# A two-layer graph kernel: x centred by TensorE, the residual kept transposed, and every other block transfer issued by GpSimd into slots of its own

## The chip, the cores and the metric

The kernel runs on one core of one Trainium2 chip. The metric is the device time in microseconds (us) of one launch; lower is better. The kernel before is timed in three runs, and one more execution of it is profiled.

## The reference, cut to what matters

N = 8192 nodes have 64 features each. The dense matrix `adj` is 8192 x 8192 float32 (256 MiB) and is used in both layers.

```
h = max(layernorm(x), 0)
x = x + adj @ (h * (u >= 0.1) / 0.9)        # layer 1
h = max(layernorm(x), 0)
x = x + adj @ (h @ W) + b                   # layer 2
```

Layer 2 needs the finished rows of layer 1: its right-hand side for a block of nodes exists only when layer 1 has been summed over the whole row of `adj` for these nodes.

## The kernel before

`adj` is cut into 16 x 16 blocks of 512 x 512 (1024 KB each). Multiplication is done with the features as the stationary operand (128 nodes x 64 features, one half of TensorE's columns) and a piece of a block as the moving one, so that two matmuls, one for each half, run side by side. Row 0 of blocks is done as two half rows of 256 nodes. W is applied at the end, to the sums of layer 2 (`acc`), and not to h.

The order of all the work is a list of 335 **items** that `Order` builds when the program is made; it is numbered from 0. An item of kind `one` is one block (or the half blocks of a pair) for layer 1 and has 2 steps; `ahead` is half a block for both layers and has 2 steps; `both`, `pair` and `mix` do two matmuls of 512 columns for each of four tiles and have 4 steps. Items 0 to 11 are half-row items of row 0 (the first unit of layer 1 is items 0 to 7), item 12 is the first that needs features of layer 2.

A block is not always used once: loaded blocks that are near the diagonal are kept for layer 2. The list of items yields a list of 341 **loads**, numbered from 0 in the order of their first use. `plan` gives each load one of the `SLOTS` places in SBUF: the one whose holder was last used earliest.

```python
    for load in loads:
        load.slot = min(range(SLOTS), key=lambda q: free[q])
        load.before, load.arrived = holder[load.slot], 16 * count[load.slot]
```

SyncE (SP) issues x and u in three parts each, then all loads in their order. Before a load into a slot that had a holder, it waits until TensorE has done the last item that uses the holder (`used`). TensorE waits before the first item of a load until the load has arrived (`block_arrived`). So a load has between its issue and its first use the work of the items between these two; this is called its **lead** here. Queue and list are in order: a load that waits for its slot holds back the ones behind it.

VectorE (DVE), ScalarE (ACT) and GpSimd (POOL) normalise x in nine groups of nodes (mean on DVE, centring on POOL, squares on ACT, the rest on DVE), which gives `features[:, :, 0:64]`. After each unit of layer 1 `unit_of_layer_1` turns the sums back to nodes by rows, adds them to `rows` and makes the features of layer 2 (`h2_ready`). `add_sum` moves finished sums out of PSUM. At the end `finish` multiplies `acc` by W for each of eight pairs of rows.

Of the kernel before, what the change touches and what calls it, by code (L numbers as in the profile page):

```python
# [4 lines left out]
P = 128  # L5
N = 8192
# [12 lines left out]
SLOTS = 14  # L19
# [8 lines left out]
GROUPS = [(0, 1), (1, 2)] + [(k, k + 2) for k in range(2, BLOCKS, 2)]  # L28

PARTS = [(0, 2), (2, 8), (8, BLOCKS)]  # L30
PART_OF = [[n for n, (a, b) in enumerate(PARTS) if a <= k0 < b][0] for k0, _ in GROUPS]
GROUP_OF = {k: g for g, (k0, k1) in enumerate(GROUPS) for k in range(k0, k1)}
BIAS_ROW = 8
# [205 lines left out]
def plan():  # L239
# [11 lines left out]
    for load in loads:  # L251
        load.slot = min(range(SLOTS), key=lambda q: free[q])
# [37 lines left out]
    for q in sorted(sums, key=lambda q: q.last):  # L290
# [3 lines left out]
        q.opens, q.ahead_opens = not halves & opened, q.ahead is not None and q.ahead not in ahead_done  # L294
# [20 lines left out]
def bass_gnn(nc, x, adj, u, w, b, out):  # L315
# [7 lines left out]
    first_ahead = min(ahead_done) // 2  # L323
    joined_by = {s: n + 1 for n, s in enumerate(sorted(ahead_done))}
    END = len(items)

# [11 lines left out]

    def unit_tiles(m):

        return slice(m * HALF_TILES, (m + 1) * HALF_TILES) if m < HALVES else slice((m - 1) * TILES, m * TILES)
# [4 lines left out]
    with ExitStack() as ctx:  # L346
# [9 lines left out]
        rows = sb("rows", [P, N // P, D])  # L356
# [3 lines left out]
        ahead = sb("ahead", [P, max(ahead_done) // 2 - first_ahead + 1, BLK])  # L360
        sums_sb = sb("sums_sb", [D, 2, BLK])
        folded = sb("folded", [D, BLK])

        w_twice = sb("w_twice", [P, D])
        bias = sb("bias", [P, D])

        eps = sb("eps", [P, 2])
        total = sb("total", [P, N // P])
# [4 lines left out]
        dev2 = sb("dev2", [P, TILES])  # L373
        centred2 = sb("centred2", [P, TILES, D])
# [3 lines left out]

        u_sb = acc[:, :, :].rearrange("p a (t d) -> p (a t) d", d=D)
        centred = features[:, :, D:2 * D]  # L380
        x_squares = features[:, :, 0:D]
# [4 lines left out]
        squares = finished[0:D, 0, :]  # L386
        banks = ctx.enter_context(nc.psum_tensor("banks", [P, SUM_BANKS, BLK], f32))

# [4 lines left out]
        bias_arrived = sem("bias_arrived")  # L393
        cleared = sem("cleared")
        warm = sem("warm")
        x_mean = sem("x_mean")
        x_centred = sem("x_centred")
        x_squared = sem("x_squared")
        x_dev = sem("x_dev")
# [26 lines left out]
        def tiles_of(k):  # L426
            return slice(k * TILES, (k + 1) * TILES)

        def group_tiles(g):
            return slice(GROUPS[g][0] * TILES, GROUPS[g][1] * TILES)  # L430

# [443 lines left out]
```

## Time and profile before

| | |
|---|---|
| median of 3 runs | 922.01 us (921.55 to 922.12) |
| profiled execution, its own time | 921.98 us |
| its span, first to last instruction | 920.2 us |
| TensorE busy | 891.7 us (97% of the span) |
| VectorE, ScalarE, GpSimd busy | 261.0, 41.0, 10.6 us |
| HBM read | 360.78 MB, 394 GB/s over the span |
| granted clock of TensorE | 1.000 |

The time of a run holds the span and 1.8 us around it. TensorE is busy in nearly all of the span, so what can be lost or won quickly is the time in which it waits. Matmul durations in rows overlap each other, because they are pipelined and two run side by side; the pace is read from the starts.

### The profile page before, as it was taken

The page shows a single profiled execution, that of the slowest core. Times are in us where ns is not written, and L with a number is a line of the kernel's source. Part 1 is how long each engine was busy: PE and PEld are TensorE (multiplying, and loading weights), DVE is VectorE, ACT ScalarE, POOL GpSimd, SP SyncE. Part 2 cuts the span into 40 slices and gives each one's busy share as a digit, 9 for nine tenths or more (in the row PEclk, how much of TensorE's full clock was granted, in tenths as well). Part 3 has the DMA queues.
Part 4 walks back from the last instruction along what each step waited for, and adds up shares of the span by engine and source line. Part 5 has one row for each costly group of instructions (what it writes and reads, how often), then busy time and mean ns, then how long its engine had stood idle before and what let it go on. Part 6 is the DMA issues. An engine that isn't in the chain of part 4 may idle for free.

```text
span 920.2 us, 10857 instructions
## 1 busy us (share of the span) xinstructions
PE 891.7 (97%) x4616; PEld 408.7 (44%) x4616; DVE 261.0 (28%) x529; ACT 41.0 (4%) x173; POOL 10.6 (1%) x18
## 2 busy tenths in 40 slices
PE   1899999999999999999999999999999999999998
PEld 1545444444444444444444444444444444444443
DVE  6664733323303303030403022030130300300423
ACT  7400000000000000000000000000000000000000
POOL 3100000000000000000000000000000000000000
PEclk9999999999999999999999999999999999999999
DMA  9999999999999999999999999999999999999996
GB/s 360 420 422 421 421 420 421 421 421 363 421 422 420 421 420 420 421 420 415 366 412 376 379 372 389 373 361 402 352 358 371 382 404 398 384 385 406 402 423 240
DMA packets 53200, 363.59 MB, mean 395 GB/s; under 512 B 5744, under 2 KB 6288, under 8 KB 11040
## 3 DMA queue, kind: packets, MB, share of 16 engines
q1 hardware_dynamic: 53056, 362.83, 97.5%
q8 instruction: 37, 0.61, 0.3%
q0 software_dynamic: 96, 0.07, 0.0%
q14 instruction: 11, 0.09, 0.0%
HBM read 360.78 MB, written 2.10 MB: 394 GB/s over the span
## 4 chain that ended last, share of the span: by engine, by line
PE 92%; DMA 6%; SPq 2%; issue 0%; DVE 0%
PE banks L737 45%; PE row_sums L713 37%; DMA blocks<-in_adj 6%; PE banks L731 6%; PE banks L747 3%; SPq L454 1%; PE row_sums L722 1%; PE banks L826 0%; PE finished L795 0%; PE row_sums L795 0%; SPq L437 0%; SPq L436 0%; DVE acc L661 0%; DVE rows L670 0%
## 5 line engine op out<-in xcount | busy, mean ns | idle before, releaser
L737 PE MATMUL banks<-blocks,features 128*64 128x512 f32 x1912 | 665.2, 593 | 0.0
L713 PE MATMUL row_sums<-blocks,features 128*64 128x512 f32 x1696 | 547.8, 592 | 2.0 <-DMA blocks<-in_adj 1.9
L737 PEld LDWEIGHTS banks<-blocks,features 128*64 128x64 f32 x1912 | 221.2, 137 | 214.0 <-issue 213.2
L713 PEld LDWEIGHTS row_sums<-blocks,features 128*64 128x64 f32 x1696 | 192.1, 137 | 203.4 <-issue 195.4
L621 DVE TENSOR_TENSOR acc<-acc,banks 64x512 f32<-64x512 f32 (+1 forms) x112 | 76.9, 687 | 575.5 <-PE banks L737 527.9
L731 PE MATMUL banks<-blocks,features 128*64 128x512 f32 x224 | 98.1, 592 | 0.1
L722 PE MATMUL row_sums<-blocks,features 128*64 128x256 f32 x256 | 32.1, 403 | 23.4 <-DMA blocks<-in_adj 23.4
L747 PE MATMUL banks<-blocks,features 128*64 128x256 f32 x240 | 54.3, 379 | 0.0
L731 PEld LDWEIGHTS banks<-blocks,features 128*64 128x64 f32 x224 | 30.6, 137 | 29.0 <-issue 28.8
L747 PEld LDWEIGHTS banks<-blocks,features 128*64 128x64 f32 x240 | 32.8, 137 | 21.6 <-issue 8.4
L589 DVE TENSOR_TENSOR rows<-rows,finished 32x128 f32<-32x128 f32 (+1 forms) x136 | 37.0, 272 | 4.3
L722 PEld LDWEIGHTS row_sums<-blocks,features 128*64 128x64 f32 x256 | 21.8, 145 | 33.6 <-DVE features L551 20.2
L520 ACT ACTIVATE sums_sb<-row_sums 64x512 f32<-64x512 f32 (+1 forms) x10 | 5.5, 552 | 378.2 <-PE row_sums L713 173.3
L493 ACT ACTIVATE features<-rows,total 128x64 f32<-128x64 f32 x64 | 21.3, 334 | 5.3 <-DVE total L533 5.3
L520 ACT ACTIVATE sums_sb<-ahead 64x512 f32<-64x512 f32 x7 | 4.4, 627 | 344.9 <-DVE ahead L636 344.9
L628 DVE TENSOR_TENSOR ahead<-ahead,banks 64x512 f32<-64x512 f32 x28 | 19.2, 686 | 0.9
L636 DVE TENSOR_TENSOR ahead<-ahead,row_sums 64x512 f32<-64x512 f32 x15 | 10.3, 685 | 21.7 <-PE row_sums L713 21.5
L619 DVE COPY acc<-banks 64x512 f32<-64x512 f32 x16 | 11.0, 689 | 17.7 <-PE banks L737 10.9
L493 ACT ACTIVATION_READ_ACCUMULATOR features<-rows,total 128x1 f32 x64 | 11.9, 186 | 0.0
L583 DVE STREAM_TRANSPOSE finished<-folded 64x512 f32<-64x512 f32 (+1 forms) x17 | 11.7, 687 | 0.6
L542 DVE SCALAR_TENSOR_TENSOR acc<-acc,square 128x512 f32<-128x512 f32 (+1 forms) x9 | 10.8, 1203 | 0.3
L626 DVE COPY ahead<-banks 64x512 f32<-64x512 f32 x15 | 10.3, 688 | 0.5
(40 smaller groups left out, 112.9 us busy)
## 6 DMA issues: line engine op xcount, KB each, us to landing
blocks<-in_adj SPq DMA_DIRECT2D x339, 1024.0 KB, 9.9
out<-rows SPq DMA_DIRECT2D x7, 256.0 KB, 5.6
rows<-in_x SPq DMA_DIRECT2D x1, 1024.0 KB, 11.5
acc<-in_u SPq DMA_DIRECT2D x1, 1024.0 KB, 13.5
blocks<-in_adj SPq DMA_DIRECT2D x2, 512.0 KB, 22.4
rows<-in_x SPq DMA_DIRECT2D x1, 768.0 KB, 7.7
acc<-in_u SPq DMA_DIRECT2D x1, 768.0 KB, 9.5
rows<-in_x SPq DMA_DIRECT2D x1, 256.0 KB, 3.2
```

Of the source, the lines that this page charges most:

```text
L493: nc.scalar.activation(x_squares[:, j, :], rows[:, j, :], ACT.Square, bias=total[:, j:j + 1], accum_out=square[:, j:j + 1]).then_inc(x_squ ...
L542: nc.vector.scalar_tensor_tensor(out=u_sb[:, t, :], in0=u_sb[:, t, :], scalar=DROP, in1=square[:, t].unsqueeze(2).to_broadcast([P, t.stop ...
L583: nc.vector.transpose(squares[:, 0:width(m)], folded[:, 0:width(m)]).then_inc(row_turned, 1)
L589: nc.vector.tensor_tensor(to, to, part[:, :, a, :], ALU.add).then_inc(row_placed, 1)
L619: nc.vector.tensor_copy(mine, banks[at, q.bank, :]).then_inc(sum_added, 1)
L621: nc.vector.tensor_tensor(mine, mine, banks[at, q.bank, :], ALU.add).then_inc(sum_added, 1)
L628: nc.vector.tensor_tensor(mine, mine, banks[at, q.bank, :], ALU.add).then_inc(sum_added, 1)
L713: return nc.tensor.matmul(row_sums[at, t.unit % 2, nodes], features[:, k * TILES + j, 0:D], tile, start=first and t.n == unit_first[t.unit ...
L722: done = nc.tensor.matmul(row_sums[half * D:(half + 1) * D, t.unit % 2, 0:HALF_BLK], features[:, t.k * TILES + j, 0:D], blocks[:, load.slo ...
L731: return nc.tensor.matmul(banks[at, t.sum.bank, nodes], features[:, t.k * TILES + j, 0:D], tile, start=j == t.tiles[0], stop=j == t.tiles[-1])
L737: return nc.tensor.matmul(banks[at, t.sum.bank, nodes], features[:, t.k * TILES + j, D:2 * D], tile, start=t.n == t.sum.first and j == t.t ...
L747: nc.tensor.matmul(banks[0:D, t.sum.bank, nodes], features[:, t.k * TILES + j, D:2 * D], tile, start=j == 0, stop=j == TILES - 1)
```

## The change

The list of items and the list of loads stay as they are. What changes:

- **Queues and slots.** There are 16 slots in place of 14. Loads with an even number go to even slots and are issued by SP, loads with an odd number go to odd slots and are issued by POOL on its own DMA queue, after its set-up. x and u stay on SP's queue, ahead of load 0.
- **Centring.** x comes in transposed (`x1`). TensorE multiplies each 128 x 128 tile of it by a centring matrix, which POOL makes at the start; this turns the tile and takes off the mean in one matmul. 32 of these stand ahead of item 0 in TensorE's program. ACT squares from PSUM in one instruction for 512 columns, DVE sums the squares; POOL's centring, DVE's means and ACT's 64 small squares go.
- **The transposed residual.** The sums of layer 1 are added to `x1` as they are (two adds), then turned into `turned` for the norm; four of the eight placing copies are done by ACT. The buffer `ahead`, its joining adds and ACT's copy of the upper sums go. The bias is added by ACT.
- **Finishing.** A pair is finished with 4 matmuls of 256 columns with W stationary, in place of 16 of 64 columns.

```diff
-SLOTS = 14
+SLOTS = 16
...
     free, holder, count = [-1] * SLOTS, [None] * SLOTS, [0] * SLOTS
-    for load in loads:
-        load.slot = min(range(SLOTS), key=lambda q: free[q])
+    for n, load in enumerate(loads):
+        load.slot = min(range(n % 2, SLOTS, 2), key=lambda q: free[q])
...
+        def load_blocks(engine, turn):
+            for load in loads[turn::2]:
                 if load.before is not None:
-                    sp.wait_ge(used, load.before.until + 1)
+                    engine.wait_ge(used, load.before.until + 1)
...
-                sp.dma_start(to, of).then_inc(block_arrived[slot], 16)
+                engine.dma_start(to, of).then_inc(block_arrived[slot], 16)
...
+            for n, (p0, p1) in enumerate(PARTS):
+                t = slice(2 * p0 * TILES, 2 * p1 * TILES)
+                sp.dma_start(x1[:, p0:p1, :], x[:, p0:p1, :]).then_inc(x_arrived[n], 16)
+                sp.dma_start(u_sb[:, t, :], u[:, t, :]).then_inc(u_arrived[n], 16)
+            load_blocks(sp, 0)
...
+            nc.gpsimd.memset(centring[:, :], 0.0).then_inc(centring_made, 1)
+            pool.wait_ge(centring_made, 1)
+            for n in range(2):
+                half = centring[(1 - n) * D:(2 - n) * D, n * D:(n + 1) * D]
+                nc.gpsimd.memset(half, -1.0 / D).then_inc(centring_made, 1)
+            for n in range(2):
+                pool.wait_ge(centring_made, 3 + n)
+                nc.gpsimd.affine_select(out=centring[:, :], in_=centring[:, :], compare_op=ALU.not_equal,
+                                        fill=1.0 - 1.0 / D, base=(2 * n - 1) * D, pattern=[[-1, 2 * D]],
+                                        channel_multiplier=1).then_inc(centring_made, 1)
+            load_blocks(pool, 1)
...
             def unit_of_layer_1(m):
-                dve.wait_ge(row_copied, m + 1)
                 dve.wait_ge(used, max(unit_last[m]) + 1)
-                lower = row_sums[0:D, m % 2, 0:width(m)]
-                if s in ahead_done:
-                    dve.wait_ge(row_joined, joined_by[s])
-                    if s % 2 == 1:
-                        lower = ahead[0:D, s // 2 - first_ahead, :]
+                if s:
+                    dve.wait_ge(sum_added, ahead_done[s])
+                link2(nc.vector.tensor_tensor(sums_of_row, sums_of_row, row_sums[0:D, m % 2, 0:width(m)], ALU.add))
+                nc.vector.tensor_tensor(sums_of_row, sums_of_row, row_sums[D:P, m % 2, 0:width(m)], ALU.add)\
+                    .then_inc(row_summed, 1)
+                dve.wait_ge(row_summed, m + 1)
                 if m:
-                    dve.wait_ge(row_turned, m)
-                nc.vector.tensor_tensor(folded[:, 0:width(m)], lower, sums_sb[:, m % 2, 0:width(m)], ALU.add)\
-                    .then_inc(row_folded, 1)
-                dve.wait_ge(row_folded, m + 1)
-                if m:
-                    dve.wait_ge(row_placed, m * (D // SQ) * (P // SQ))
-                nc.vector.transpose(squares[:, 0:width(m)], folded[:, 0:width(m)]).then_inc(row_turned, 1)
+                    dve.wait_ge(row_placed, m * (P // SQ))
+                    dve.wait_ge(row_placed_act, m * (P // SQ))
+                nc.vector.transpose(squares[x1_half(s), 0:width(m)], sums_of_row).then_inc(row_turned, 1)
                 dve.wait_ge(row_turned, m + 1)
-                for f in range(D // SQ):
-                    part = squares[f * SQ:(f + 1) * SQ, 0:width(m)].rearrange("p (t a f) -> p t a f", t=tiles, f=SQ)
-                    for a in range(P // SQ):
-                        to = mine[a * SQ:(a + 1) * SQ, :, f * SQ:(f + 1) * SQ]
-                        nc.vector.tensor_tensor(to, to, part[:, :, a, :], ALU.add).then_inc(row_placed, 1)
-                dve.wait_ge(row_placed, (m + 1) * (D // SQ) * (P // SQ))
+                base = x1_half(s).start
+                part = squares[base:base + SQ, 0:width(m)].rearrange("p (t a f) -> p t a f", t=tiles, f=SQ)
+                for a in range(P // SQ):
+                    nc.vector.tensor_copy(turned[a * SQ:(a + 1) * SQ, 0:tiles, 0:SQ], part[:, :, a, :])\
+                        .then_inc(row_placed, 1)
...
-                    mine = ahead[at, q.p - first_ahead, :]
-                    if q.ahead_opens:
-                        nc.vector.tensor_copy(mine, banks[at, q.bank, :]).then_inc(sum_added, 1)
-                    else:
-                        nc.vector.tensor_tensor(mine, mine, banks[at, q.bank, :], ALU.add).then_inc(sum_added, 1)
-            def join_ahead(m):
-                s = row_of(m)
-                at = slice((1 - s % 2) * D, (2 - s % 2) * D)
-                dve.wait_ge(used, max(unit_last[m]) + 1)
-                dve.wait_ge(sum_added, ahead_done[s])
-                mine = ahead[at, s // 2 - first_ahead, :]
-                nc.vector.tensor_tensor(mine, mine, row_sums[at, m % 2, :], ALU.add).then_inc(row_joined, 1)
+                    mine = x1[at, q.p, :]
+                    nc.vector.tensor_tensor(mine, mine, banks[at, q.bank, :], ALU.add).then_inc(sum_added, 1)
...
-            def finish(n, p, tiles):
-                for j in tiles:
-                    for half in range(2):
-                        for row in range(2):
-                            at, nodes = slice(half * D, (half + 1) * D), j * P + half * D
-                            mine = slice(row * D, (row + 1) * D)
-                            done = nc.tensor.matmul(final_banks(n)[at, row, j * D:(j + 1) * D],
-                                                    acc[mine, p, nodes:nodes + D], w_twice[mine, :],
-                                                    start=True, stop=True)
-                done.then_inc(finished_ready, 1)
+            def finish(n, r, c, bank, acc_of):
+                return nc.tensor.matmul(final_banks(n)[c * D:(c + 1) * D, bank, 0:acc_of.shape[1]],
+                                        w_twice[r * D:(r + 1) * D, 0:D], acc_of, start=True, stop=True)
...
+            pe.wait_ge(centring_made, 5)
+            for p in range(PAIRS):
+                pe.wait_ge(x_arrived[PART_OF[p]], 16)
+                if p >= len(centred):
+                    pe.wait_ge(xd_ready, p - len(centred) + 1)
+                for j in range(TILES):
+                    done = nc.tensor.matmul(x_centred_of(p)[:, 2 * j:2 * j + 2, :], x1[:, p, j * P:(j + 1) * P],
+                                            centring[:, :], start=True, stop=True)
+                done.then_inc(x_centred, 1)
```

On TensorE the matmuls of the centring stand at the start of the program. `centring` is the matrix, `x` is the transposed input, `row_sums` takes the sums of layer 1. Before:

```order
L722 MATMUL row_sums<-blocks,features 64x256 [waits block_arrived0,xd_ready]
L722 MATMUL row_sums<-blocks,features 64x256 x7
L722 MATMUL row_sums<-blocks,features 64x256 [waits block_arrived1,xd_ready]
L722 MATMUL row_sums<-blocks,features 64x256 x7
L722 MATMUL row_sums<-blocks,features 64x256 [waits block_arrived2,xd_ready]
```

and in the changed kernel, from the last two pairs of rows that are centred:

```order
L833 MATMUL row_sums<-centring,x 128x128 [waits x_arrived2]
L833 MATMUL row_sums<-centring,x 128x128 x3
L833 MATMUL banks<-centring,x 128x128 [waits xd_ready,x_arrived2]
L833 MATMUL banks<-centring,x 128x128 x3
L710 MATMUL row_sums<-blocks,features 64x256 [waits block_arrived0,xd_ready]
L710 MATMUL row_sums<-blocks,features 64x256 x7
L710 MATMUL row_sums<-blocks,features 64x256 [waits block_arrived1,xd_ready]
```

32 matmuls in groups of four have come in ahead of the first item, the last groups behind the third part of x (`x_arrived2`); the 8 matmuls of each half-row item and their waits are the same.

On SP the program of before begins like this (`rows` and `acc` take x and u, `blocks` the loads):

```order
L436 DMA rows<-in_x 128x512
L437 DMA acc<-in_u 128x512
L436 DMA rows<-in_x 128x1536
L437 DMA acc<-in_u 128x1536
L436 DMA rows<-in_x 128x2048
L437 DMA acc<-in_u 128x2048
L454 DMA blocks<-in_adj 128x2048 x12
L454 DMA blocks<-in_adj 128x1024
```

In the changed kernel SP has the same six, and then only half of the loads:

```order
L468 DMA acc<-in_u 128x2048
L461 DMA blocks<-in_adj 128x2048 x6
L461 DMA blocks<-in_adj 128x1024
L461 DMA blocks<-in_adj 128x2048
L461 DMA blocks<-in_adj 128x2048 [waits used] x7
```

The other half of the loads stands on POOL, behind the making of the centring matrix:

```order
L485 DMA w_twice<-in_wb 64x65
L488 MEMSET centring 128x128
L492 MEMSET centring 64x64 [waits centring_made]
L495 AFFINE_SELECT centring<-centring 128x128
L495 AFFINE_SELECT centring<-centring 128x128 [waits centring_made]
L461 DMA blocks<-in_adj 128x2048 x8
L461 DMA blocks<-in_adj 128x2048 [waits used] x72
```

POOL's first eight loads (1, 3, ... 15) wait for nothing but POOL itself, and x and u are not ahead of them in its queue.

What the two ways of giving out slots do to single loads can be listed from `plan`. The steps of lead are those of the items between the release of the slot (or that of a load ahead of it in its queue, if later) and the first use:

```
load  first used   before: released   steps     changed: released   steps
      by item      after item         of lead   after item          of lead
 80      95           88               12          91                  6
 82      97           91               12          93                  8
 92     108          100               16         106                  2
 94     110          105                8         108                  2
 96     113          107               14         110                  8
108     126          119               14         122                  8
110     128          122               14         124                  8
loads with 8 steps or fewer:            1                              7
loads with 12 steps or fewer:          14                             15
```

## Rows read from the trace of the kernel before

**Rows 1.** The page: span, busy time, the share of the main queue

```profile
span 920.2 us, 10857 instructions
PE 891.7 (97%) x4616; PEld 408.7 (44%) x4616; DVE 261.0 (28%) x529; ACT 41.0 (4%) x173; POOL 10.6 (1%) x18
```

**Rows 2.** Busy time by stretch: PE, PEld, DVE, ACT, POOL, clock, DMA share, GB/s

```profile
0.00:10.00 10.00, 0.00 (x0) 0.00 (x0) 2.92 (x8) 4.84 (x20) 2.73 (x10) 1.00 0.79 274
20.00:30.00 10.00, 9.50 (x70) 6.27 (x68) 9.48 (x16) 9.38 (x54) 3.33 (x4) 1.00 1.01 422
130.00:140.00 10.00, 9.36 (x44) 3.45 (x42) 4.48 (x12) 0.59 (x1) 0.00 (x0) 1.00 1.02 424
140.00:150.00 10.00, 9.46 (x53) 4.60 (x51) 2.82 (x7) 0.30 (x1) 0.00 (x0) 1.00 1.01 422
250.00:260.00 10.00, 9.17 (x44) 2.96 (x44) 1.29 (x4) 0.30 (x1) 0.00 (x0) 1.00 1.01 421
300.00:400.00 100.00, 100.00 (x485) 45.74 (x483) 23.50 (x53) 2.41 (x5) 0.57 (x1) 1.00 1.01 420
800.00:900.00 100.00, 100.00 (x570) 45.36 (x568) 24.06 (x50) 1.19 (x3) 0.00 (x0) 1.00 0.99 401
```

**Rows 3.** The waits of all engines: who waited for whom

```profile
PE row_sums L722 <- DMA blocks<-in_adj: 23.4, 9, 19.2
PE row_sums L713 <- DMA blocks<-in_adj: 1.9, 4, 0.6
```

**Rows 4.** The timeline of PE from 0 to 60 us

```profile
19.20 9.45 PE L722 MATMUL row_sums<-blocks,features 128*64 128x256 f32 x64 [19.20 <-DMA blocks<-in_adj]
29.15 1.95 PE L722 MATMUL row_sums<-blocks,features 128*64 128x256 f32 x16 [0.50 <-DMA blocks<-in_adj]
...
44.04 1.95 PE L722 MATMUL row_sums<-blocks,features 128*64 128x256 f32 x16 [0.52 <-DMA blocks<-in_adj]
46.53 1.95 PE L722 MATMUL row_sums<-blocks,features 128*64 128x256 f32 x16 [0.54 <-DMA blocks<-in_adj]
48.27 0.59 PE L731 MATMUL banks<-blocks,features 128*64 128x512 f32 x1
```

**Rows 5.** The line that issues the loads: time from issue to landing

```profile
L454 SPq DMA_DIRECT2D blocks<-in_adj x341: 327/328/6210, 3.7 to 887.4; - x171
DMA to landing us min/median/max: 4.7/9.9/29.8
```

**Rows 6.** The chain that ended last, 115 to 150 and 205 to 260 us

```profile
143.67 0.21 PE banks L747
...
205.54 1.72 PE row_sums L713 x8
...
245.07 7.85 DMA blocks<-in_adj
252.96 1.94 PE row_sums L713 x8
```

**Rows 7.** DMA view of 0 to 50 us (40 slices of 1.25 us), and a small transfer of POOL's

```profile
GB/s 0 116 264 327 349 363 362 415 419 433 419 426 433 426 426 433 419 426 426 419 419 426 419 419 419 419 419 433 419 419 426 419 413 406 400 446 410 423 419 419
...
bias<-in_b POOLq DMA_DIRECT2D x1, 32.0 KB, 5.3
```

**Rows 8.** The timeline of POOL and of DVE: the set-up, and the last features of a unit

```profile
1.94 0.53 POOL L474 DMA_DIRECT2D w_twice<-in_w  x1
...
22.89 1.04 POOL L480 TENSOR_TENSOR features<-rows,total 128x512 f32<-128x512 f32 x1 [2.23 <-DVE total L533]
...
142.21 0.42 DVE L604 SCALAR_TENSOR_TENSOR features<-centred,square 128x256 f32<-128x256 f32 x1
```

**Rows 9.** The groups by line with shapes apart: a weight load and an add

```profile
L713 PEld LDWEIGHTS row_sums<-blocks,features 128*64 128x64 f32 x1696 | 192.1, 137 | 203.4 <-issue 195.4 <-DMA blocks<-in_adj 6.8
L621 DVE TENSOR_TENSOR acc<-acc,banks 64x512 f32<-64x512 f32 x49 | 33.6, 685 | 190.6 <-PE banks L737 143.2 <-PE row_sums L713 47.4
```

**Rows 10.** The timeline of the end, 880 to 920 us

```profile
894.49 0.69 PE L795 MATMUL row_sums<-w_twice,acc 64*64 64x64 f32 x32
...
895.11 3.65 PE L737 MATMUL banks<-blocks,features 128*64 128x512 f32 x16
...
898.70 0.69 PE L795 MATMUL finished<-w_twice,acc 64*64 64x64 f32 x32
```

More of the change, by code:

```diff
@@ L27 @@
 STEP, BLOCK_LOAD, LANDING, MARGIN, H2_LEAD, ROW_LEAD = 0.858, 2.49, 1.6, 8.0, 8.0, 10.0
[L28 to L33, printed above, removed]
+PARTS = [(0, 1), (1, 4), (4, PAIRS)]
+PART_OF = [n for n, (p0, p1) in enumerate(PARTS) for _ in range(p0, p1)]
 SQ = 32
@@ L293, in plan @@
         assert not halves & opened or halves <= opened
-        q.opens, q.ahead_opens = not halves & opened, q.ahead is not None and q.ahead not in ahead_done
+        q.opens = not halves & opened
         opened |= halves
@@ L322, in bass_gnn @@
     final_end = {pair_end[p]: p for p in finals}
-    first_ahead = min(ahead_done) // 2
-    joined_by = {s: n + 1 for n, s in enumerate(sorted(ahead_done))}
     END = len(items)
+    assert sorted(ahead_done) == list(range(1, BLOCKS))
     last = items[-1]
@@ L355, in bass_gnn @@
         features = sb("features", [P, N // P, 2 * D])
-        rows = sb("rows", [P, N // P, D])
+        x1 = sb("x1", [P, PAIRS, BLK])
         acc = sb("acc", [P, PAIRS, BLK])
[L360 to L365, printed above, removed]
+        centring = sb("centring", [P, 2 * D])
+        w_twice = sb("w_twice", [P, D + 1])
+        bias = w_twice[:, D:D + 1]
         eps = sb("eps", [P, 2])
-        total = sb("total", [P, N // P])
         square = sb("square", [P, N // P])
@@ L487, in _ @@
+            for n in range(2):
[4 more added lines that the diff above has]
+            load_blocks(pool, 1)
         @block.scalar
         def _(act):
-            def squares_x(g):
-                act.wait_ge(x_mean, 2 * g + 2)
-                for j in range(GROUPS[g][0] * TILES, GROUPS[g][1] * TILES):
-                    nc.scalar.activation(x_squares[:, j, :], rows[:, j, :], ACT.Square, bias=total[:, j:j + 1],
-                                         accum_out=square[:, j:j + 1]).then_inc(x_squared, 1)
@@ L595, in unit_of_layer_1 @@
                 nc.vector.tensor_reduce(var, power, AX.X, ALU.add).then_inc(h2_summed, 1)
-                if s == BIAS_ROW:
-                    dve.wait_ge(bias_arrived, 16)
-                if s >= BIAS_ROW:
-                    since = rows[:, slice(0 if s == BIAS_ROW else s * TILES, (s + 1) * TILES), :]
-                    nc.vector.tensor_tensor(since, since, bias[:, :].unsqueeze(1).to_broadcast(
-                        [P, since.shape[1], D]), ALU.add).then_inc(biased, 1)
                 dve.wait_ge(h2_dev, m + 1)
```

226 lines of the change are left out of this document (115 added, 111 removed).

## The prediction

> **What bounds the kernel now.** I read the page first, then the busy time by stretch, the waits of TensorE, and last the places where it waits. The page shows TensorE busy in 891.7 of 920.2 us [rows 1]; by stretch it is at 100.00 of 100 us from 300 us on [rows 2]. So the change can win only in the other 28 us, but it can lose anywhere. Nearly all of TensorE's waiting is on transfers of blocks [rows 3]: 19.2 us until load 0, then a gap in front of each of the items 1 to 11, and four small ones later. In the timeline items 10 and 11 start at 44.04 and 46.53, 2.49 us apart [rows 4], while such an item is 1.72 us of work [rows 6]. 2.49 us is 1024 KB (1.049 MB) at the 422 GB/s of the stretch, where the share of the DMA engines is 1.01 [rows 2]: the transfers are the bound up to 48.27 us, where item 12 starts. From there TensorE has no reserve: its shortfall is 0.64 and 0.54 us at 130 to 150 us and 0.83 us at 250 to 260 us [rows 2], and none later. The reader should take this from it: **whatever makes the first twelve items late by more than about 1.2 us moves the end by the rest, and every new gap behind them moves it by its whole length.**
>
> The last gap has another cause than the first ones. The chain goes from an item that ended at 245.07 through a transfer of 7.85 us to the next item at 252.96 [rows 6]: load 94, with a lead of 8 steps, that is 4 items of 1.72 us, 6.9 us. Its slot came free too late. That is the measure for the table of leads: a load needs 4.7 us from issue to landing at the least, of 341 of them [rows 5], and 7.85 us where others are in flight.
>
> **The start.** SP must bring x and u (4096 KB, 4.19 MB) and then loads 0, 2, ... 10. Up to load 10 that is 4.19 + 6 x 1.049 = 10.49 MB. Before, load 11 needed 4.19 + 12 x 1.049 = 16.78 MB. First I test the working on this: by 6.25 us the first five slices give 1.25 us x (0 + 116 + 264 + 327 + 349) GB/s = 1.32 MB [rows 7]; (16.78 - 1.32) / 0.422 = 36.6 us; 6.25 + 36.6 = 42.9, and the item starts at 46.53 [rows 4], 3.6 us later. That is the lag between the bytes and TensorE (by the same working of load 0 it is 3.7 us).
>
> POOL's set-up ends at 2.5 us [rows 8]; behind it stand three small fills and two selects over 128 columns, each of which I take as at most the 1.04 us of POOL's instruction on 512 columns [rows 8], and the first transfer needs some time to start. I let POOL's queue join at 6.25 us (bounds 4 and 9 us). It has 8 free slots and nothing ahead of them, and its slots are freed again from item 3 on, so it has work all the time. If the engines serve both queues alike, SP gets 211 GB/s. Load 0 is then there at 6.25 + 3.92/0.211 + 3.6 = 28.4 us in place of 19.2, and load 10 at 6.25 + 9.17/0.211 + 3.6 = 53.3 us. Items 10 and 11 are 3.44 us more: item 12 starts at 56.7 us in place of 48.27, **+8.4 us**. The blocks that POOL has brought in meanwhile are of no use to a TensorE that needs the even ones in order. It doesn't depend much on the shares: with a third for POOL, its sixth load (load 11, 6.29 MB at 141 GB/s) is the late one, 6.25 + 44.6 + 3.6 = 54.5 us, and item 12 starts at 56.2.
>
> Do both queues share? POOL's 32 KB transfer of the bias landed in 5.3 us [rows 7], while a block on SP's queue took 9.9 us at the median behind its own kind [rows 5]; it did not stand behind what SP had issued. The Trainium skill says the same ("DMA: Bandwidth & Descriptors", "Queues, rings and completion order": each engine goes round the queues that have work, packet by packet). By that rule the start costs the 8.4 us; by the order of issue it would cost nothing. The same page ("Issuing engines are not separate DMA queues") says that issuing from several engines saves only the issue time; the share of 1.01 with one queue [rows 2] agrees, so I count no gain in rate.
>
> Of the 8.4 us about 1.2 are taken up by the two gaps between 130 and 150 us: **-1.2**.
>
> **The slots.** Loads 92 and 94 have 2 steps of lead, 1.72 us. Each is issued when a TensorE that is one item away from it frees the slot, and no work done elsewhere hides that. The gap is the landing less 1.72 us: 3.0 us with the least landing, 6.1 us with 7.85 us [rows 5, 6]. POOL's queue will be in flight beside it and TensorE's standstill empties the queues, so I take the middle, 4.5 us: **+9.0**. Load 80 has 6 steps, 5.2 us: 0 to 2.7 us, taken as **+1.0**. Four loads (82, 96, 108, 110) have 8 steps, the lead with which load 94 waited 0.8 us before: 0 to 1 us each, **+1.0** together, since two of them come behind gaps in which the queue has caught up. Load 94's old gap goes: **-0.8**. The two further slots deepen the reserve of the odd loads, but the count of short leads goes up, and where leads are long nothing waited before [rows 3].
>
> **What I cost at nothing.** The 32 centring matmuls: the last 16 follow the third part of x, which by the working above has 3.15 MB of SP's queue: 6.25 + 1.83/0.211 + 3.6 = 18.5 us. One is at most two weight loads of 137 ns [rows 9] and a quarter of a half-row item's columns in time, 0.21 us: 16 x 0.49 = 7.8 us, until 26.3, under load 0 at 28.4. If load 0 came at 19.2 this cover would be gone, and the first item would start up to 2.8 us late (x at 6.25 + 1.83/0.422 + 3.6 = 14.2 us, plus 7.8), which the gaps of 0.77 us in front of items 1 to 11 would take up. DVE and ACT at the front have the same cover. Later, DVE loses adds of 685 ns [rows 9] and is busy for 28% [rows 1]. The chain that makes layer-2 features loses ACT's copy and four placings and gains an add; it ended at 142.63 us, 1.0 us before the item that began at 143.67 [rows 6, 8], and with TensorE later in that stretch for want of nothing else, this can cost 0 to 0.5 us. The finishing of a pair takes 0.62 us from its first matmul to the next item (894.49 to 895.11) [rows 10]; four matmuls of 256 columns are two times 0.43 us if they run in twos (8 of them are 1.72 us, [rows 6]), 0.43 if all four do: -0.2 to +0.2 us for each of eight. I take 0.
>
> **Sum.** 8.4 - 1.2 + 9.0 + 1.0 + 1.0 - 0.8 = +17.4 us on the span of 920.2: 937.6. The profiled execution took 921.98, 1.8 us more than its span and as much as the median 922.01; so 939.4 us, 939 in round numbers.
>
> **The rivals.**
> *Served in order of issue (0.15).* If POOL's transfers queue behind what SP has issued before, the start costs nothing and no gap is taken up: 9.0 + 1.0 + 1.0 - 0.8 = +10.2, 932 us; with the least landings 6.0 - 0.8 = +5.2, 927 us. For it: one set of engines. Against it: the 5.3 us.
> *POOL's turns are larger, or its issues come late (0.13).* With two thirds for POOL, load 0 comes at 6.25 + 3.92/0.141 + 3.6 = 37.7 us, and the 12 items of 1.72 us then run to 58.3: +10.0. Beside such a queue the gaps are at their upper bounds, 12.2 + 2.7 + 4.0 - 0.8. With -1.2 that is +26.9, 949 us. A transfer issue was 0.53 us of POOL for 64 partitions [rows 8], and these have 128, some 1.1 us by that; the 171 of them have 5.3 us each, so POOL must be held up for long to matter. The Trainium skill knows a way ("SBUF — State Buffer", "SBUF: two separate sides", the box on DVE and DMAs issued from GpSimd: an SBUF-to-SBUF float32 copy of DVE keeps GpSimd from writing descriptors); the copies here read PSUM, and no run shows it.
> *Not slower: two queues move more than one (0.04).* At 600 GB/s, load 10 would come at 6.25 + 9.17/0.3 + 3.6 = 40.4 us, item 12 start at 43.9 (-4.4), and landings would be some 1.5 us shorter, gaps 2 x 3.0 - 0.8 and none for the others: +0.8 us, 923 us. From there on the kernel is not slower. It needs 42% more than 422 GB/s, and the highest slice is 446 [rows 7].
>
> **How the numbers follow.** The forecast, both terms present, has 0.68 and its own range from 933 to 946 us (gaps of 3.0 or 6.1 us, POOL joining at 9 us or 4 us). The range of 929 to 948 leaves out the lower part of the first rival, the upper part of the second and the third. A measurement of this kernel can't tell less than 0.2%, 1.8 us, from no change. Slower by more: 0.96, all of the first three cases; the third rival is split over same and faster, 0.02 each.
>
> **What the profile after would show.** TensorE's first item at about 28 us in place of 19.2, behind matmuls of the centring that end by 26; even items waiting and odd ones not, 5 us from pair to pair; item 12 at about 57 us; two gaps of 3 to 6 us at about 260 to 275 us that end with transfers on SP's queue, and a smaller one some 30 us before; then 100% again. I am wrong if the first item starts near 20 us, if the gaps at loads 92 and 94 are under 3 us, if POOL's loads land so late that TensorE waits for odd ones, or if new gaps stand behind 320 us, above all with DVE or ACT as their cause.

## The result and the profile after

The changed kernel takes **946.9 us** (median of 4 runs, 944.0 to 947.85) against 922.03: a ratio of 1.0269, 95% interval 1.0257 to 1.0281. It is slower, by 24.9 us; 17.4 us were forecast, and the range of 929 to 948 us held the time. The profiled execution is the fastest of the four, 944.0 us with a span of 942.0, 21.8 us over that of before.

The page of the changed kernel, the rows that answer to [rows 1] and its strip of transfers:

```profile
span 942.0 us, 10443 instructions
PE 905.8 (96%) x4488; PEld 414.2 (44%) x4488; DVE 234.6 (25%) x449; ACT 43.0 (5%) x120; POOL 93.0 (10%) x183
...
GB/s 359 421 421 419 421 421 422 420 421 353 394 295 401 395 383 423 376 421 407 370 383 415 377 401 358 390 341 381 385 363 355 398 381 409 390 392 399 411 420 144
```

DVE is 26 us less busy. TensorE is 14 us more busy, most of it in the new matmuls ahead of the first item, and its idle time has grown by 8 us (from 28.5 to 36.2). What this costs is read from the stages. The timeline of PE at the start, against [rows 4]:

```profile
4.60 2.05 PE L833 MATMUL banks<-centring,x 128*128 128x128 f32 x8 [4.60 <-DMA x<-in_x]
...
21.66 1.06 PE L833 MATMUL banks<-centring,x 128*128 128x128 f32 x8
27.28 8.81 PE L710 MATMUL row_sums<-blocks,features 128*64 128x256 f32 x64 [4.56 <-DMA blocks<-in_adj]
...
42.18 3.67 PE L710 MATMUL row_sums<-blocks,features 128*64 128x256 f32 x32 [1.30 <-DMA blocks<-in_adj]
47.16 3.67 PE L710 MATMUL row_sums<-blocks,features 128*64 128x256 f32 x32 [1.30 <-DMA blocks<-in_adj]
52.13 3.67 PE L710 MATMUL row_sums<-blocks,features 128*64 128x256 f32 x32 [1.30 <-DMA blocks<-in_adj]
55.88 0.61 PE L720 MATMUL banks<-blocks,features 128*64 128x512 f32 x1
```

The first item starts at 27.28 us, and the items come in pairs now, 4.97 us from pair to pair: the even load has just landed and the odd one lies there. Item 12 starts at 55.88 in place of 48.27, 7.6 us late. The centring ends at 22.7 us, under the wait for load 0.

Busy time by stretch, against [rows 2] (PE, PEld, DVE, ACT, POOL, clock, DMA share, GB/s):

```profile
55.00:215.00 160.00, 159.93 (x798) 73.12 (x796) 68.98 (x113) 3.76 (x12) 15.86 (x30) 1.00 1.01 420
215.00:240.00 25.00, 22.46 (x111) 9.14 (x108) 7.59 (x16) 2.10 (x6) 3.17 (x6) 1.00 0.91 362
240.00:280.00 40.00, 31.80 (x141) 11.55 (x138) 7.57 (x16) 2.08 (x6) 2.64 (x5) 0.91 0.87 331
300.00:320.00 20.00, 16.57 (x77) 6.14 (x74) 3.44 (x9) 1.39 (x4) 1.58 (x3) 1.00 0.99 370
320.00:900.00 580.00, 580.00 (x2784) 260.49 (x2782) 105.79 (x209) 23.00 (x66) 57.48 (x108) 1.00 0.97 389
```

Between 55 and 215 us nothing is lost; the two gaps of before at 130 to 150 us are gone. Everything else is lost between 215 and 320 us. There the share of the DMA engines falls to 0.91 and 0.87: transfers are not issued, for want of a slot. From 320 us on TensorE is at 100%. The chain over this stretch, against [rows 6], has each late landing with its length. Its first line is the item that began at 205.54 us before:

```profile
210.84 1.72 PE row_sums L701 x8
...
224.61 9.55 DMA blocks<-in_adj
234.20 3.65 PE row_sums L701 x16
...
243.10 11.04 DMA blocks<-in_adj
254.18 1.96 PE row_sums L701 x8
256.16 6.27 DMA blocks<-in_adj
262.48 3.71 PE row_sums L701 x8
266.20 4.72 DMA blocks<-in_adj
270.97 1.94 PE row_sums L701 x8
...
305.62 10.44 DMA blocks<-in_adj
```

At 210.84 us TensorE is 5.3 us late, against 7.6 us at item 12: the gaps of before have taken up 2.3 us. 256.16 is the end of item 106, 262.48 the start of item 108: load 92 landed 6.27 us after its slot came free, of which item 107 covers 1.72. 266.20 is the end of item 108: load 94 landed after 4.72 us, the least that a load takes. And item 108 took 3.71 us where the items around it take 1.94 to 1.96: in this stretch TensorE's granted clock is below 1.00.

### The profile page after: what moved, and what is told of

Its sections match the earlier page's. It is cut to its first block, busy times and chain, and to the rows that moved or that the text cites. A ratio compares the mean times of both kernels' runs of the same rounds, so it can differ in the third digit from the quotient of the medians.

```text
span 942.0 us, 10443 instructions
## 1 busy us (share of the span) xinstructions
PE 905.8 (96%) x4488; PEld 414.2 (44%) x4488; DVE 234.6 (25%) x449; ACT 43.0 (5%) x120; POOL 93.0 (10%) x183
## 4 chain that ended last, share of the span: by engine, by line
PE 90%; DMA 9%; SPq 1%; issue 0%; DVE 0%
PE banks L726 43%; PE row_sums L701 37%; DMA blocks<-in_adj 9%; PE banks L720 5%; PE banks L736 3%; PE row_sums L710 1%; PE banks L813 0%; SPq L461 0%; PE finished L778 0%; PE row_sums L778 0%; SPq L468 0%; SPq L467 0%; DVE x L660 0%
## 5 line engine op out<-in xcount | busy, mean ns | idle before, releaser
L461 POOL DMA_DIRECT2D blocks<-in_adj x170 | 90.4, 532 | 808.5 <-PE banks L726 596.6
L530 ACT ACTIVATE turned<-finished 32x128 f32<-32x128 f32 (+1 forms) x68 | 17.8, 262 | 812.3 <-DVE finished L590 811.1
L627 DVE TENSOR_TENSOR x<-x,banks 64x512 f32<-64x512 f32 x43 | 29.5, 686 | 1.3
L581 DVE TENSOR_TENSOR x<-x,row_sums 64x512 f32<-64x512 f32 (+1 forms) x17 | 11.0, 650 | 43.1 <-PE row_sums L701 21.5
L595 DVE COPY turned<-finished 32x128 f32<-32x128 f32 (+1 forms) x68 | 18.8, 277 | 2.2
L621 DVE COPY acc<-banks 64x512 f32<-64x512 f32 x16 | 11.0, 689 | 19.4 <-PE banks L726 11.6
L833 PE MATMUL banks<-centring,x 128*128 128x128 f32 x40 | 8.6, 399 | 6.7 <-DMA x<-in_x 6.7
L590 DVE STREAM_TRANSPOSE finished<-x 64x512 f32<-64x512 f32 (+1 forms) x17 | 11.8, 693 | 0.6
L535 ACT ACTIVATE x<-x,w_twice 64x512 f32<-64x512 f32 (+1 forms) x17 | 11.8, 694 | 0.4
L582 DVE TENSOR_TENSOR x<-x,row_sums 64x512 f32<-64x512 f32 (+1 forms) x17 | 11.2, 660 | 0.6
L833 PEld LDWEIGHTS banks<-centring,x 128*128 128x128 f32 x40 | 7.9, 302 | 6.9 <-POOL centring L495 4.6
## 6 DMA issues: line engine op xcount, KB each, us to landing
blocks<-in_adj SPq DMA_DIRECT2D x2, 512.0 KB, 37.7
```

The source lines that it names most:

```text
L461: engine.dma_start(to, of).then_inc(block_arrived[slot], 16)
L530: nc.scalar.activation(turned[a * SQ:(a + 1) * SQ, 0:tiles, SQ:D], part[:, :, a, :], ACT.Copy)\
L535: nc.scalar.activation(x1_of(m), x1_of(m), ACT.Identity, bias=bias[x1_half(s), :]).then_inc(biased, 1)
L595: nc.vector.tensor_copy(turned[a * SQ:(a + 1) * SQ, 0:tiles, 0:SQ], part[:, :, a, :])\
L627: nc.vector.tensor_tensor(mine, mine, banks[at, q.bank, :], ALU.add).then_inc(sum_added, 1)
L833: done = nc.tensor.matmul(x_centred_of(p)[:, 2 * j:2 * j + 2, :], x1[:, p, j * P:(j + 1) * P], centring[:, :], start=True, stop=True)
```

## The experiments

Each kernel is the changed one with the edit shown. Kernels that ran together share their runs of the kernel before: its median is 921.1 us for `all_sp`, `free_slots2`, `sp_free16` and `pool_late`, 922.2 us for `sp_free14`, `pool_after12`, `pool_after12_par` and `fill`, and 921.4 us for `after_again`, `pool_after60` and `pool_after60_par`. Across these groups the ratios are compared.

| kernel | slots | POOL issues | median, us | ratio to before, interval |
|---|---|---|---|---|
| changed | even and odd | odd loads | 946.9 | 1.0269 (1.0257 to 1.0281) |
| after_again | even and odd | odd loads | 945.9 | 1.0264 (1.0248 to 1.0280) |
| all_sp | even and odd | none | 931.5 | 1.0105 (1.0091 to 1.0118) |
| free_slots2 | any of 16 | odd loads | 927.7 | 1.0068 (1.0054 to 1.0082) |
| sp_free16 | any of 16 | none | 920.0 | 0.9984 (0.9976 to 0.9993) |
| sp_free14 | any of 14 | none | 922.0 | 0.9997 (0.9987 to 1.0006) |
| pool_late | even and odd | odd loads, after u | 944.7 | 1.0266 (1.0239 to 1.0293) |
| pool_after12 | any of 16 | odd loads from 12 on | 933.4 | 1.0121 (1.0107 to 1.0135) |
| pool_after12_par | even and odd | odd loads from 12 on | 953.0 | 1.0324 (1.0308 to 1.0341) |
| pool_after60 | any of 16 | odd loads from 60 on | 925.3 | 1.0040 (1.0025 to 1.0055) |
| pool_after60_par | even and odd | odd loads from 60 on | 945.8 | 1.0271 (1.0240 to 1.0303) |
| fill | even and odd | odd loads | 945.1 | 1.0258 (1.0224 to 1.0291) |

**The two parts apart.** `all_sp` keeps the slots and gives all loads to SP:

```diff
-            for load in loads[turn::2]:
+            for load in loads:
...
-            load_blocks(pool, 1)
```

Expected: 

> The changed kernel with all 341 loads issued by SP in their order; the even and odd slots stay as they are. Theory 1 (the lateness at the start, +7.6 us, is two queues sharing the engines while x and u stand on one of them; the gaps near 230 to 316 us, +14.3 us, are the short leads of the even and odd slots): the first item is back near 19.2 us and item 12 near 48.3, the gaps before items 108 and 110 stay at 3 to 4.5 us each, and the time is 927 to 933 us. Theory 2 (the gaps come from POOL's queue being in flight or being slow): the gaps go with the queue, 921 to 924 us. Theory 3 (the other parts of the change cost several us as well): over 934 us.

Measured: 931.5 us. Items 0 to 11 are 2.48 us apart again, item 11 at 45.49 us. The gaps stay. The chain of `all_sp`:

```profile
246.75 4.77 DMA blocks<-in_adj
...
253.54 4.76 DMA blocks<-in_adj
```

Loads 92 and 94 land 4.8 us after their slots come free, near the least of 4.7 us, and are late all the same: from the end of item 106 (246.75) to item 110 (258.35) 11.6 us go by with three items of 1.72 us in them, 6.4 us are lost. Theory 1 holds, theory 2 falls: the gaps don't need POOL's queue. They are shorter without it: the same stretch is 14.8 us in the changed kernel, 9.6 us lost. And this although by `plan` ten loads of `all_sp` have 8 steps of lead or fewer, not seven, because in one queue a load that waits for its slot holds back the odd ones too. What POOL's queue was doing there can be read from the timelines of SP and of POOL in the changed kernel:

```profile
256.16 0.33 SPq L461 DMA_DIRECT2D blocks<-in_adj  x1
```

```profile
253.67 0.53 POOL L461 DMA_DIRECT2D blocks<-in_adj  x1 [2.90 <-PE row_sums L701]
258.15 0.53 POOL L461 DMA_DIRECT2D blocks<-in_adj  x1 [3.95 <-PE row_sums L701]
```

The line of SP is load 92. The two of POOL are loads 101 and 103, first used by items 119 and 121; they landed 6.1 and 6.9 us after their issues, at 259.8 and 265.1 us. So both were in flight while TensorE stood before item 108 and waited for load 92.

`free_slots2` keeps the queue and gives up even and odd slots. A slot can be filled from both queues there, so each queue counts its arrivals in a semaphore of its own.

```diff
-        load.slot = min(range(n % 2, SLOTS, 2), key=lambda q: free[q])
+        load.slot = min(range(SLOTS), key=lambda q: free[q])
+        load.sem = 2 * load.slot + n % 2
```

Expected: 

> The changed kernel with POOL still issuing the odd loads, but every load may take any of the 16 slots, that with the longest free one first (semaphores for each slot and queue). Theory 1: the start stays late (item 12 near 56 us), the gaps at 225 to 320 us are under 1 us each and the clock does not fall there, 928 to 931 us. Theory 2: the gaps stay, 940 us or more.

Measured: 927.7 us. Busy time by stretch of `free_slots2`:

```profile
230.00:250.00 20.00, 20.00 (x103) 9.60 (x101) 1.53 (x3) 0.00 (x0) 1.59 (x4) 1.00 1.01 423
250.00:260.00 10.00, 10.00 (x50) 4.45 (x48) 6.03 (x14) 2.09 (x6) 1.59 (x3) 1.00 1.01 420
260.00:270.00 10.00, 10.00 (x50) 4.42 (x48) 0.69 (x1) 0.00 (x0) 1.06 (x2) 1.00 1.01 422
```

No gap and no fall of the clock in this stretch, with as many loads issued by POOL as in the changed kernel. The clock did fall at the start: in this execution the last pair of half-row items waited 2.83 us, took 5.36 us in place of 3.67, and item 12 started at 58.94 us, 3 us later than in the changed kernel's profile (the first item at 27.40 is as there). It is the slowest execution of the four. The median is 0.3 us below what theory 1 expected; theory 2 falls.

**What is left without both.** `sp_free16` has both edits, `sp_free14` also `SLOTS = 14`.

```diff
-SLOTS = 16
+SLOTS = 14
```

Expected of sp_free16: 

> The changed kernel with all loads on SP and free choice among 16 slots, so that only the centring, the transposed residual, the finishing and two more slots are left of the change. Theory 1: these cost nothing and win at most the 0.8 us gap at 253 us and some tenths at the end, 920.5 to 922.5 us. Theory 3: over 924 us.

Expected of sp_free14: 

> The changed kernel with all loads on SP, free choice among 14 slots as in the kernel before. If the 1.1 us that 16 slots with these parts won come from the gap of load 94 (0.8 us, lead of 8 steps with 14 slots): 921 us. If they come from the other parts: 920 us.

Measured: 920.0 us, 1.1 us under before, with an interval that leaves out 1; and 922.0 us, no difference. The centring, the transposed residual and the finishing cost nothing and win nothing that can be told. The small win fits the two more slots, whose share of the stretch 240 to 260 us can be seen: TensorE is busy for 18.69 of 20 us with 14 slots and 20.00 with 16. The two intervals touch, so the times alone don't show it. By its ratio `sp_free14` is at the 921 us that were expected if the slots make the win.

So against `sp_free16` the queue alone costs 7.7 us, the slots alone 11.5, both together about 26 (0.9984 to 1.0269 is 2.85% of 922, 26.3 us; by `after_again` it is 25.8). Some 7 us belong to neither alone.

**Where the queue costs.** `pool_late` lets POOL wait for the last part of u:

```diff
+            pool.wait_ge(u_arrived[len(PARTS) - 1], 16)
             load_blocks(pool, 1)
```

Expected: 

> The changed kernel, but POOL waits with its first load until the last part of u has landed (about 16.5 us), so that x, u and load 0 have the engines to themselves. Theory 1 (sharing by equal turns): the first item is at about 19 to 20 us, then TensorE waits for load 1 instead (about 24 us) and for odd loads from then on; item 12 starts at 52 to 55 us, and the gaps of the slots stay; 938 to 944 us. If sharing were not the cause of the late start, item 12 would stay at 56 us and the time at 944 to 948 us.

Measured: 944.7 us, 0.7 us over what theory 1 expected and inside the other range; its interval holds the changed kernel's ratio. Item 0 starts at 18.91 us, but item 1 at 26.55. The timeline of PE in `pool_late`, items 12 and 13:

```profile
52.71 0.59 PE L721 MATMUL banks<-blocks,features 128*64 128x512 f32 x1
...
55.92 0.61 PE L721 MATMUL banks<-blocks,features 128*64 128x512 f32 x1 [1.30 <-DMA blocks<-in_adj]
```

Item 12 starts at 52.71 us, inside what theory 1 expected and 3.2 us ahead of the changed kernel. Item 13 then waits for POOL's load 13 and is 1.7 us ahead (55.92 against 57.6). In this execution load 92 landed 8.74 us after its slot came free, 2.5 us more than in the changed kernel's, and took that lead away for a while; the spans are 940.3 and 942.0 us, and the medians can't be told apart. So sharing with x and u is a small part of what the start costs, some 1.7 of 7.6 us. For the rest it only decides which of the two queues is late. `pool_after12` gives the first twelve loads to SP (`pool_after12_par` is the same with even and odd slots):

```diff
+        load.turn = n % 2 if n >= 12 else 0
...
-            for load in loads[turn::2]:
+            for load in [load for load in loads if load.turn == turn]:
```

Expected of pool_after12: 

> Any of 16 slots for any load, loads 0 to 11 all on SP, and from load 12 on odd loads on POOL. If the queue costs only by sharing the engines with x, u and the first twelve loads: item 12 starts near 48.3 us and the time is 920 to 922 us, as with all loads on SP. If a second queue costs later too (loads that come in pairs, POOL's issues, writes of descriptors beside DVE's work): 923 us or more, with waits of TensorE behind 60 us.

Expected of pool_after12_par: 

> Even and odd slots as in the changed kernel, loads 0 to 11 all on SP, from load 12 on odd loads on POOL. The even and odd slots cost 11.5 us with all loads on SP; with both the slots and the queue the cost is 26 us, against 7.7 and 11.5 apart. If the missing 7 us lie in the gaps of the short leads, which POOL's transfers in flight make longer: 937 to 941 us. If they lie in the start: 930 to 933 us.

Measured: 933.4 and 953.0 us, both worse than POOL from the start. The first has the time of the rival (923 us or more), but through waits in front of items 1 to 12; the second lies above both of its ranges. The timeline of POOL in `pool_after12` says why:

```profile
4.26 1.09 POOL L463 DMA_DIRECT2D blocks<-in_adj  x2 [0.17 <-issue]
34.47 0.53 POOL L463 DMA_DIRECT2D blocks<-in_adj  x1 [29.11 <-PE row_sums L712]
39.44 0.53 POOL L463 DMA_DIRECT2D blocks<-in_adj  x1 [4.44 <-PE row_sums L712]
49.28 0.53 POOL L463 DMA_DIRECT2D blocks<-in_adj  x1 [9.32 <-PE row_sums L712]
54.32 0.53 POOL L463 DMA_DIRECT2D blocks<-in_adj  x1 [4.51 <-PE row_sums L712]
```

The timeline of PE there, item 11:

```profile
60.45 1.95 PE L712 MATMUL row_sums<-blocks,features 128*64 128x256 f32 x16 [3.02 <-DMA blocks<-in_adj]
```

POOL had loads 13 and 15 in flight from 4.3 us on, and four more as slots came free. Item 11 starts at 60.45 us and not at 45.58 as in `sp_free16`, its match with all loads on SP: 14.9 us, or 6.0 blocks of 2.49 us, for the six blocks that POOL brought and nobody needed yet. The same count fits the changed kernel. By an estimate from the pace of its pairs, POOL moves a block each 4.97 us from 6.25 to 53 us, 9.4 blocks, of which six are among the first twelve; 3.4 x 2.49 = 8.5 us, and item 12 starts 8.6 us later than in `sp_free16` (55.88 against 47.33; 7.6 against the kernel before). It does not cover `free_slots2`, whose item 12 is 3 us later still: what makes its last pair wait 2.83 us is open. **What the second queue costs is the bytes that it moves ahead of their turn while TensorE waits for others.**

Last, `pool_after60` and `pool_after60_par` make the switch where the start is long over (`n >= 60`):

Expected of pool_after60: 

> Any of 16 slots for any load; loads 0 to 59 all on SP, from load 60 on the odd ones on POOL, where each waits for its slot. In the run with the switch at load 12 POOL had issued loads 13 and 15 at 4.3 us and 17, 19 and so on as slots came free, so that item 12 came at 62 us: this says that a block of POOL's which is not needed yet costs 2.49 us at the start. Theory 1 (the queue costs only there): item 12 at 48.3 us, 919 to 921.5 us, as with all loads on SP (920.0). Rival (the second queue costs later too): 923 us or more.

Expected of pool_after60_par: 

> Even and odd slots, loads 0 to 59 on SP, from load 60 on the odd ones on POOL: the start of all loads on SP, and both queues where the short leads stand. With all loads on SP these slots cost 11.5 us (931.5). Theory 1a (POOL's transfers in flight make the landings of loads 80 to 110 longer, and the clock falls in the longer gaps; this is the 7 us by which the two parts together cost more than their sum): 935 to 940 us. Rival (the 7 us belong to the start): 930 to 933 us.

Measured: 925.3 and 945.8 us. `pool_after60` by stretch:

```profile
150.00:200.00 50.00, 45.75 (x204) 18.17 (x202) 12.33 (x18) 0.00 (x0) 3.70 (x7) 0.97 1.01 421
200.00:240.00 40.00, 40.00 (x198) 17.27 (x196) 12.40 (x23) 2.10 (x6) 4.23 (x8) 1.00 0.96 387
330.00:880.00 550.00, 550.00 (x2644) 250.74 (x2642) 98.23 (x193) 20.91 (x60) 54.34 (x102) 1.00 0.98 392
```

The theory that the queue costs only at the start is wrong as I put it, and the rival (923 us or more) has the time. TensorE stands for 4.25 us between 150 and 200 us, with the engines at a share of 1.01: at the switch. POOL gets ahead of SP, which has a backlog there: POOL's loads 61, 63, 65 and 67 had landed by 173.2 us, while load 60 on SP's queue, which item 75 waited for, landed at 177.55. These are two waits, of 0.92 and 3.33 us, the second with a fall of the clock behind it (0.97 over the stretch), and none after them, though POOL issues half of the loads from there on. In steady flow the second queue costs nothing. `pool_after60_par` lies above both of its ranges: with even and odd slots the same kernel takes 20.5 us more (945.8 to 925.3), where these slots cost 11.5 us with all loads on SP; from `free_slots2` to the changed kernel it is 18 to 19 us. The starts of the same matmuls in two profiles say where: between 212 and 301 us of `sp_free16`, `all_sp` loses 11.2 us against it, the changed kernel 17.9, `after_again` 20.4 and `pool_after60_par` 20.5, and `free_slots2` loses nothing. So the missing 7 us are in the gaps of the short leads, which are longer when POOL issues loads beside them. They are not in the start.

**Variation and the clock.**

Expected of after_again: 

> The changed kernel once more, on the same chip as the two others. 943 to 948 us as before. In the profiled executions of this kernel and its relatives item 10 started at 52.13 us in one and at 53.77 us in two others with the same start of the program; if that is what spreads the times of the changed kernel over 4 us, the execution profiled here has one or the other, and a time to match (944 or 946 to 948 us).

Measured: 945.9 us, the profiled execution 945.2 of span. Item 10 started at 52.83 us, neither of the two values of the expectation. That is 0.7 us later than in the first profile, of the 3.2 us by which the span is longer, so the start makes little of the spread. The chain of `after_again` has another difference:

```profile
256.74 10.27 DMA blocks<-in_adj
...
270.73 4.86 DMA blocks<-in_adj
```

Load 92 took 10.27 us to land here and 6.27 in the first profile: 4.0 us between two executions of one kernel, as large as the spread of its times (944.0 to 947.85). The same loads of POOL, 101 and 103, were in flight beside it in both. What sets the one or the other is open.

`fill` puts eight spare matmuls in front of the waits for loads 92 and 94:

```diff
+                if t.n in (108, 110):
+                    for j in range(8):
+                        half = j % 2
+                        nc.tensor.matmul(finished[half * D:(half + 1) * D, 1, :], features[:, 0, 0:D],
+                                         features[:, 0:TILES, :], start=True, stop=True)
                 arrived(t)
```

Expected: 

> The changed kernel with eight spare matmuls of 512 columns (their sums go to a bank of PSUM that nothing reads) on TensorE ahead of the wait for load 92 and again ahead of the wait for load 94. They are 3.4 us of work each time. If the clock falls because TensorE stands still there, the stretch 260 to 270 us keeps its full clock, item 108 takes 1.9 us in place of 3.7, and the time is 1.5 to 3.5 us below that of the changed kernel: 943 to 945 us. If the fall has nothing to do with the standstill, the clock falls as before and the time is 946 to 948 us. Were the spare matmuls longer than the waits, 948 us or more.

Measured: 945.1 us, interval 1.0224 to 1.0291, which holds the changed kernel's 1.0269: inconclusive in time. The timeline of PE in `fill`:

```profile
258.08 3.60 PE L758 MATMUL finished<-features 128*64 128x512 f32 x16
263.68 5.35 PE L701 MATMUL row_sums<-blocks,features 128*64 128x512 f32 x16 [2.00 <-DMA blocks<-in_adj]
268.86 3.60 PE L758 MATMUL finished<-features 128*64 128x512 f32 x16
272.29 1.89 PE L701 MATMUL row_sums<-blocks,features 128*64 128x512 f32 x8
```

The 2.00 us that are left of the first wait were followed by a slow item again (two items in 5.35 us, 3.65 being usual); behind the second filling there is no idle time and the item takes its 1.89 us. In the stretch 260 to 270 us the granted clock is 0.83 and in the changed kernel 0.66. The expectation that item 108 keeps its full speed missed; the run doesn't show how short a rest must be for that.

## Why the prediction was right, and where its sizes were off

Both mechanisms of the forecast are there and stand where it put them. That the time lies inside the range owes something to the width of the range: the slots cost half as much again as their terms, and the fall of the clock was not in them at all.

**What bounds the kernel**: right. Beyond the gaps of before, TensorE has no reserve behind item 12, and the end moved by what the start and the slots lost: 7.6 us at item 12 and 14.2 between it and the end make the 21.8 us of the spans.

**The start**: +8.4 forecast, +7.6 measured; load 0 at 28.4 forecast, 27.28 measured. Equal turns are shown by the pairs of items 4.97 us apart. The Trainium skill ("DMA: Bandwidth & Descriptors", "Queues, rings and completion order") has the engines go round the queues with work, and the trace agrees. Its advice in the same page ("Issuing engines are not separate DMA queues"), that issuing from several engines saves only issue time, agrees with 420 to 422 GB/s with one queue and with two. But my reason, that SP has x and u ahead of its loads, was too narrow: `pool_late` took that away and won back 1.7 us at item 13, and `pool_after12` cost more with x, u and the first twelve loads all on SP. It is the order of the bytes that counts. The rival by order of issue (932 us) is out. So is the one of larger turns or late issues: the first item starts at 27.28 us and not at 37.7, and an issue of POOL's took 0.53 us for 128 partitions as for 64, and not the 1.1 us that I had scaled it to.

**The gaps that take up lateness**: -1.2 forecast, -2.3 measured (7.6 us late at item 12, 5.3 at 210.84). The forecast counted only the shortfall of 1.18 us at 130 to 150 us, which is gone.

**The slots** are the mis-sized term: +11.0 (9.0 + 1.0 + 1.0), less 0.8, was forecast, 10.2 net. From 210.84 us to the end the profiled execution lost 21.8 - 5.3 = 16.5 us. The 4.5 us each for loads 92 and 94 were near: 4.6 us by the landing of 6.27, and 3.0 by that of 4.72. The idle time in front of item 110 is only 2.74 us in the timeline, and a gap under 3 us at load 94 was one of my signs of being wrong; by the landing, 4.72 less 1.72 us, it is 3.0. Too small were the others. Loads 80 and 82 brought 1.84 and 0.69 us of idle time, load 90 (12 steps of lead, not in my list) another 0.82, loads 108 and 110 the two of 1.32 and 2.10 us behind 305 us: 6.8 us where I had 2.0, and between the starts of items each is some 0.2 us longer. I had taken 7.85 us as the longest landing, from a kernel with one queue; here 9.55, 11.04 and 10.44 us stand in the chain. And item 108 took some 1.8 us more at the lower clock, which the forecast did not have at all. The median is 3 us above this execution. The spread of the landing of load 92 is as large, but two profiles don't show that it is the cause.

**What I cost at nothing** did cost nothing that can be told: the finishing has a period of 4.2 us before and after, `sp_free14` is at 0.9997.

What is shown is that the two parts cost 7.7 and 11.5 us alone and the rest by meeting, and that the rest lies in the gaps of the short leads. That the landings are longer because POOL's blocks, sent ahead of their turn, share the engines with the awaited one is the reading that fits (4.77 us with one queue, 6.27 and 10.27 with two, for the same load, with loads 101 and 103 in flight). No run took it apart from other causes, and it doesn't say why one execution has 6.27 and the other 10.27.

## What to carry to other kernels

A kernel that waits for transfers in a fixed order wants them in that order. The second queue added no bytes per second here, and each block that it brought before its turn delayed the one that was waited for by its whole time, 2.49 us. When slots are given out under an extra rule, count the work between the release of each slot and the first use of what goes into it, and compare the smallest with the least time of a transfer, 4.7 us here. In the changed kernel seven of 341 loads have 8 steps of lead or fewer. With all loads on SP the rule for slots cost 11.5 us, where the change without it and without the second queue won 1.1. Two such costs don't simply add: together they cost 7 us more than their sum.

## What the runs showed of the hardware

TensorE's granted clock fell in the changed kernel, which it did not in the one before, whose rows in [rows 2] all say 1.00. Busy time by stretch of the changed kernel:

```profile
20.00:30.00 10.00, 5.44 (x36) 4.55 (x37) 9.66 (x19) 2.77 (x7) 0.00 (x0) 0.84 1.01 421
...
260.00:270.00 10.00, 5.75 (x16) 1.52 (x16) 0.00 (x0) 0.00 (x0) 0.53 (x1) 0.66 0.68 242
```

Of its two levels, 2.4 and 1.2 GHz, the lower was granted for a part of these stretches. In the changed kernel this came with rests of TensorE of 3.06, 4.56 and 4.64 us, each of which followed work; the item after the last took 3.71 us in place of 1.94. At the start this is hidden by transfers; at 262 us it is paid in full. So a wait here can cost its own length and up to 2 us more. The length of the rest alone does not tell when. The rests of 2.74 and 2.10 us in the same execution were followed by items at full speed (1.94 us), but in `after_again` the item behind a rest of 1.92 us took 3.09 us, and in `fill`, with spare work up to a rest of 2.00 us, the next two took 5.35 in place of 3.65. With no rest the next item ran at full speed.
